# A four-batch mixture-of-experts kernel: the next batch's routing among a batch's last three tiles, its exponentials behind the first two evictions of x

## The reference, cut to what matters

```
# x (4, 1024, 1024) f32, side (4, 1024, 1), cond (4, 1024); E = 8 experts, F = 128, R = 16, top 2
def cond_ref(side, cond, x, k):                 # k = 10240, for each of 16 (here 4) matrices
    att = softmax(x, axis=-1) / sqrt(1024)
    adj = side * cond[:, None, :] * att
    adj[:, diag, diag] = -inf
    return 1.0 at the k largest entries of each matrix, 0.0 elsewhere
def ffn(m):                                     # m: the 0/1 mask of above, (4, 1024, 1024)
    scores = softmax(m @ G); w = top-2 of scores, at their experts
    gated = silu(m @ gate_w[e].T) * (m @ up_w[e].T)
    out  = sum over e of w[e] * gated @ down_w[e].T
    out += sum over e of w[e] * (m @ lora_A[e].T) @ lora_B[e].T
    return out
result = x + ffn(cond_ref(side, cond, x, 10240))
```

## Time and profile before

| | us |
|---|---|
| median of three runs | 833.69 |
| lowest and highest | 831.17, 837.47 |
| the profiled execution | 836.23 |
| its span, first to last instruction | 834.5 |
| mean granted TensorE clock, as a share of full | 0.838 |

### The profile page before, as it was taken

How to read it: one execution, slowest core, us unless ns; L and a number is a source line. 1 busy time by engine, 2 the same in 40 slices (tenths; PEclk the granted TensorE clock), 3 DMA queues, 4 the chain that set the end, 5 groups by cost and what they waited for, 6 DMA issues and landing times.

```text
span 834.5 us, 14610 instructions
## 1 busy us (share of the span) xinstructions
PE 529.9 (63%) x4178; PEld 358.9 (43%) x4178; DVE 519.5 (62%) x1242; ACT 455.4 (55%) x655; POOL 388.8 (47%) x337
## 2 busy tenths in 40 slices
PE   0211376289888754787887726987788368798810
PEld 0200365156555533454555414654455146465500
DVE  5768799576778465865885676757861623233335
ACT  6686387658744564485444553874445345355510
POOL 7123200234473114487786124877871157767510
PEclk9755599589999995898899967999999869899965
DMA  9980340114232904478377734685678247767569
GB/s 315 358 234 0 115 189 26 45 55 158 88 127 86 356 28 129 147 252 288 107 263 240 319 104 148 215 287 174 212 247 334 77 131 252 268 212 264 203 234 380
DMA packets 80443, 159.93 MB, mean 192 GB/s; under 512 B 22889, under 2 KB 32105, under 8 KB 79856
## 3 DMA queue, kind: packets, MB, share of 16 engines
q1 hardware_dynamic: 59760, 108.60, 37.8%
q0 software_dynamic: 20608, 50.37, 17.3%
HBM read 107.53 MB, written 73.40 MB: 217 GB/s over the span
## 4 chain that ended last, share of the span: by engine, by line
DMA 19%; PE 18%; DVE 17%; issue 15%; POOL 14%; ACT 8%; DVEq 4%; SPq 3%; POOLq 1%; ACTq 0%
DMA out_dram<-piece 7%; DMA piece<-put_rows 6%; PE pa L676 5%; ACT mask L791 3%; DMA xg<-mask_rows,where 3%; POOL piece L526 3%; POOL piece L529 3%; DVE mask L1060 3%; DVE w L1166 2%; PE pb L663 2%; POOL xg L509 2%; ACT t_row L828 2%; DMA w<-put_rows 2%; PE pd L625 2%; POOL put_rows L517 2%
## 5 line engine op out<-in xcount | busy, mean ns | idle before, releaser
L676 PE MATMUL pa<-w,xt 128*128 x1472 | 203.2, 294 | 1.1 <-issue 0.9
L848 ACT ACTIVATE y<-pc,where 128x512 f32<-128x512 f32 x184 | 125.3, 687 | 104.8 <-PE pc L702 97.4
L676 PEld LDWEIGHTS pa<-w,xt 128*128 128x128 f16 x1472 | 150.7, 103 | 62.1 <-issue 14.7
L517 POOL DMA_INDIRECT put_rows<-y,where x92 | 92.5, 1005 | 151.9 <-ACT y L848 133.3
L1336 DVE SCALAR_TENSOR_TENSOR g_full<-pa,where,s_act 128x144 f32<-128x144 f32 x92 | 33.5, 365 | 197.0 <-ACT s_act L840 196.9
L509 POOL DMA_INDIRECT xg<-mask_rows,where x92 | 97.4, 1058 | 122.8 <-DVEq L1328 92.9
L835 ACT ACTIVATE xt<-pb 128x1024 f16<-128x1024 f16 x92 | 94.3, 1025 | 101.7 <-PE pb L663 98.7
L663 PE MATMUL pb<-ident,xg 128*128 128x128 f16 x736 | 61.4, 231 | 68.5 <-DMA xg<-mask_rows,where 46.2
L663 PEld LDWEIGHTS pb<-ident,xg 128*128 128x128 f16 x736 | 48.7, 104 | 80.1 <-DMA xg<-mask_rows,where 53.5
L840 ACT ACTIVATE s_act<-pa,small 128x128 f32<-128x128 f32 x92 | 33.8, 368 | 86.8 <-PE pa L676 86.8
L702 PE MATMUL pc<-lb,gt 128*128 x184 | 77.4, 420 | 0.0
(11 more groups left out here) (208 smaller groups left out, 880.0 us busy)
## 6 DMA issues: line engine op xcount, KB each, us to landing
piece<-put_rows SPq DMA_DIRECT2D x96, 256.0 KB
v<-in_x_dram SPq DMA_DIRECT2D x40, 512.0 KB, 9.1
piece<-in_x_dram SPq DMA_DIRECT2D x48, 256.0 KB
out_dram<-piece SPq DMA_DIRECT2D x48, 256.0 KB, 3.8
mask_rows<-mask SPq DMA_DIRECT2D x4, 2048.0 KB, 16.6
w<-put_rows SPq DMA_DIRECT2D x16, 512.0 KB, 10.2
w<-in_L_ffn_gate_w_dram SPq DMA_DIRECT2D x8, 512.0 KB, 10.2
w<-in_L_ffn_up_w_dram SPq DMA_DIRECT2D x8, 512.0 KB, 8.3
```

The lines of the kernel that those rows point to most:

```text
L517: pool.indirect_dma_start(out=put_rows[n % 2], out_offset=bass.IndirectOffsetOnAxis(ap=put_row[n][:, i:i + 1], axis=0), in_=y[:, g % NY, : ...
L676: last = pe.matmul(l1[g % 2], xt[:, g % 2, t, :], w1[:, bass.ds(e, 1), t, k, :].rearrange("p o n -> p (o n)"), start=(t == 0 and k == 0), ...
L848: nc.scalar.activation(y[:, g % NY, half * HALF:(half + 1) * HALF], pc[:, half, :], ACT.Copy, scale=y_scale[n][:, i:i + 1]).then_inc(y_rea ...
```

## The change

The search's steps move up by a third to one and a half tiles each; the turning of the mask goes from tiles 19 to 22 into tiles 17 to 19; the five parts of route get places of their own among tiles 20 to 22, with rank and place_slots on TensorE and the last score in tile 20; the probabilities go to tile 20; the maxima move to tiles 20 to 22, six of them into tile 22; the exponentials of batch n + 1 are issued at the start of batch n, behind its first two evictions of x (for n = 1 and 2); GpSimd issues the next batch's first gathers behind the put of tile 20; the sums of pieces skip tile 16, and the mask's move stands behind the load of piece 13.

```diff
--- before.py
+++ after.py
@@ -76,29 +76,36 @@
     SCALE_AT = {(0, 0): 0, (0, 1): 1, (0, 2): 2, (1, 0): 3, (1, 1): 4, (1, 2): 5, (2, 0): 6, (2, 1): 7}
     SIDE_SUM_AT = (1, 3)
     DIAG_AT = 3
-    AIM_AT = {(2, 2): 1, (5, 1): 2, (8, 0): 3, (10, 1): 4}
+    AIM_AT = {(2, 2): 1, (5, 1): 2, (7, 2): 3, (9, 2): 4}
     DVE_COUNT_AT = {(3, 1): (1, 0), (3, 2): (1, 1), (4, 0): (1, 2), (5, 2): (2, 0), (6, 0): (2, 1),
-                    (6, 1): (2, 2), (8, 0): (3, 0), (8, 1): (3, 1), (8, 2): (3, 2)}
+                    (6, 1): (2, 2), (7, 2): (3, 0), (8, 0): (3, 1), (8, 1): (3, 2)}
     ACT_COUNT_AT = {(3, 0): (1, 0), (3, 1): (1, 1), (3, 2): (1, 2), (4, 0): (1, 3), (5, 2): (2, 0),
-                    (6, 0): (2, 1), (6, 1): (2, 2), (6, 2): (2, 3), (8, 1): (3, 0), (8, 2): (3, 1),
-                    (9, 0): (3, 2), (9, 1): (3, 3)}
-    SUM_AT = {(5, 0): 1, (7, 2): 2, (10, 0): 3}
-    BELOW_AT = {10: (0, 2), 11: (4,), 12: (6, 7)}
-    DVE_BELOW_AT = {(10, 1): 1, (11, 1): 3, (12, 1): 5}
-    BEST_AT = {(10, 2): 0, (11, 0): 1, (11, 2): 2, (12, 0): 3, (12, 2): 4, (13, 0): 5, (13, 1): 6, (13, 2): 7}
-    NEAREST_AT, NEAREST_SPREAD_AT = (14, 1), (14, 3)
-    RANK_AT = {(15, 0): (0, 1), (15, 1): (2, 3)}
-    PICK_AT, PICK_SUM_AT = (15, 2), (16, 0)
-    MASK_AT = {(16, 1): (0, 1), (16, 2): (2, 3), (17, 0): (4, 5), (17, 1): (6, 7)}
-    MASK_SUM_AT = (18, 1)
-    CHECK_AT = (18, 2)
-    TURN_AT = {(19, 0): 0, (19, 2): 1, (20, 0): 2, (20, 2): 3, (21, 0): 4, (21, 2): 5, (22, 0): 6, (22, 2): 7}
-    STORE_MT_AT = dict(TURN_AT)
-    MAX_AT = {(19, 2): 0, (20, 0): 1, (20, 1): 2, (20, 2): 3, (21, 0): 4, (21, 2): 5, (22, 0): 6, (22, 2): 7}
-
-
-    PIECE_AT = {**{j + 1: j for j in range(9)}, **{j + 4: j for j in range(9, PIECES)}}
-    PIECES_FIRST = 14
+                    (6, 0): (2, 1), (6, 1): (2, 2), (6, 2): (2, 3), (8, 0): (3, 0), (8, 1): (3, 1),
+                    (8, 2): (3, 2), (9, 0): (3, 3)}
+    SUM_AT = {(5, 0): 1, (7, 1): 2, (9, 2): 3}
+    BELOW_AT = {10: (0, 2), 11: (4, 6), 12: (7,)}
+    DVE_BELOW_AT = {(10, 0): 1, (11, 0): 3, (12, 0): 5}
+    BEST_AT = {(10, 1): 0, (10, 2): 1, (11, 0): 2, (11, 1): 3, (11, 2): 4, (12, 0): 5, (12, 1): 6, (12, 2): 7}
+    NEAREST_AT, NEAREST_SPREAD_AT = (13, 0), (13, 2)
+    RANK_AT = {(14, 0): (0, 1), (14, 1): (2, 3)}
+    PICK_AT, PICK_SUM_AT = (14, 2), (15, 0)
+    MASK_AT = {(15, 1): (0, 1), (15, 2): (2, 3), (16, 0): (4, 5), (16, 1): (6, 7)}
+    MASK_SUM_AT = (16, 3)
+    CHECK_AT = (17, 0)
+    TURN_AT = {(17, 1): 0, (17, 3): 1, (18, 0): 2, (18, 2): 3, (18, 3): 4, (19, 0): 5, (19, 2): 6, (19, 3): 7}
+    STORE_MT_AT = {(17, 1): 0, (17, 2): 1, (18, 0): 2, (18, 1): 3, (18, 2): 4, (19, 0): 5, (19, 1): 6, (19, 2): 7}
+    LAST_SCORE_AT = (20, 1)
+
+    CHOOSE_AT, WEIGH_AT, PLACE_AT, TABLE_AT, SLOTS_TAKEN_AT = (20, 1), (21, 0), (21, 0), (21, 1), (22, 0)
+    PAIR_RANK_AT, SLOTS_AT = (20, 3), (22, 0)
+    PROBS_AT = (20, 2)
+
+    MAX_AT = {(20, 2): (0,), (21, 2): (1,), (22, 1): (2, 3, 4), (22, 2): (5, 6, 7)}
+    EXPS_FIRST = 0
+
+
+    PIECE_AT = {**{j + 1: j for j in range(9)}, **{j + 4: j for j in range(9, 12)}, **{j + 5: j for j in range(12, PIECES)}}
+    PIECES_FIRST = 12
 
     with ExitStack() as ctx:
         def sb(name, shape, dt):
@@ -529,11 +536,15 @@
                 nc.gpsimd.tensor_tensor(piece[:, at, 0, :], piece[:, at, 0, :], piece[:, at, 2, :],
                                         ALU.add).then_inc(summed_piece, 1)
 
-            for n in range(B):
+            def first_gathers(n):
                 pool.wait_ge(routed, n + 1)
                 pool.wait_ge(mask_stored, 16 * (n + 1))
                 for i in range(NX):
                     gather(n, i)
+
+            for n in range(B):
+                if n == 0:
+                    first_gathers(0)
                 if n >= 2:
 
                     pool.wait_ge(summed_piece, PIECES * (n - 1))
@@ -549,8 +560,11 @@
                             below_third(n + 1, q)
                     if n > 0 and i in PIECE_AT:
                         sum_piece(n - 1, PIECE_AT[i])
-                for i in range(T - 3, T):
-                    put_out(n, i)
+                put_out(n, T - 3)
+                if n + 1 < B:
+                    first_gathers(n + 1)
+                put_out(n, T - 2)
+                put_out(n, T - 1)
 
         @block.tensor
         def _(pe):
@@ -751,6 +765,12 @@
                         turn_mask(n + 1, c)
                         if c > 0:
                             score(n + 1, c - 1)
+                    if (i, spot) == LAST_SCORE_AT:
+                        score(n + 1, C - 1)
+                    if (i, spot) == PAIR_RANK_AT:
+                        rank(n + 1)
+                    if (i, spot) == SLOTS_AT:
+                        place_slots(n + 1)
 
                 for i in range(T):
                     experts[i] = load_expert(n, i)
@@ -765,15 +785,9 @@
                     if i >= 2:
                         second_layer(n, i - 2, experts[i - 2])
                     between(i, 3)
-                if more:
-                    score(n + 1, C - 1)
                 turn_g(n, T - 1)
                 second_layer(n, T - 2, experts[T - 2])
-                if more:
-                    rank(n + 1)
                 second_layer(n, T - 1, experts[T - 1])
-                if more:
-                    place_slots(n + 1)
 
         @block.scalar
         def _(act):
@@ -898,9 +912,17 @@
                         count(n + 1, k, p)
                     if more and (i, spot) in STORE_MT_AT:
                         store_mt(n + 1, STORE_MT_AT[i, spot])
+                    if more and (i, spot) == PROBS_AT:
+                        probabilities(n + 1)
+                        if n + 2 < B:
+                            for c in range(EXPS_FIRST):
+                                exponential(n + 2, c)
 
                 store_xt(n, 0)
                 store_xt(n, 1)
+                if n > 0 and more:
+                    for c in range(EXPS_FIRST, C):
+                        exponential(n + 1, c)
                 for i in range(T):
                     silu(n, i)
                     if i + 2 < T:
@@ -914,13 +936,8 @@
                     between(i, 2)
                 store_y(n, T - 2, 0)
                 store_y(n, T - 2, 1)
-                if more:
-                    probabilities(n + 1)
                 store_y(n, T - 1, 0)
                 store_y(n, T - 1, 1)
-                if n + 2 < B:
-                    for c in range(C):
-                        exponential(n + 2, c)
 
         @block.vector
         def _(dve):
@@ -1420,8 +1437,19 @@
                         make_mask(n + 1, MASK_AT[here])
                     if here == CHECK_AT:
                         check_mask(n + 1)
+                    if here == CHOOSE_AT:
+                        choose(n + 1)
+                    if here == WEIGH_AT:
+                        weigh(n + 1)
+                    if here == PLACE_AT:
+                        place_pairs(n + 1)
+                    if here == TABLE_AT:
+                        fill_table(n + 1)
+                    if here == SLOTS_TAKEN_AT:
+                        take_slots(n + 1)
                     if n + 2 < B and here in MAX_AT:
-                        maximum(n + 2, MAX_AT[here])
+                        for c in MAX_AT[here]:
+                            maximum(n + 2, c)
 
                 for i in range(T):
                     between(i, 0)
@@ -1431,8 +1459,6 @@
                         store_gt(n, i - 1)
                     between(i, 2)
                 store_gt(n, T - 1)
-                if more:
-                    route(n + 1)
 
 
             for c in range(C):
```

## The result

The kernel with the change takes 877.3 us (median of four runs, 868.4 to 880.1), the kernel before in the same comparison 832.8: a ratio of 1.051, 95% interval 1.042 to 1.060. The forecast was 856.0 with a range of 832 to 872. So the sign was right and the size was not: by the ratio it is about 42 slower, where 22 were forecast. The profiled execution took 875.1, its span 873.3; that of before had 836.2 and 834.5.

A forecast was written before the change was run, and what follows sets the result against it. An order of waits, not a full engine, was taken to bound the kernel. Boundary, search and turning +3.8, exponentials +13, pieces +2, clock and port +3 make +21.8 on 836.2, less 2.5: about 856 us, range 832 to 872.

The forecast's parts named there:

- What bounds it: Whole kernel: no engine is full, an order of waits bounds a batch; TensorE's 20.7 us stretch at three boundaries is targeted.
- From choose to the next first layer: Batch boundary: 6.2 us longer after batch 2, 9.6 after batches 0 and 1, which have maxima; 25.4 over three boundaries.
- Rival 2: Faster: exponentials vanish behind VectorE's scalings, maxima behind put and gather, boundary first layers run warm; 828.5 us, chance 0.12.
- The exponentials: Start of batches 1 and 2: they delay the first silu, tile 3 comes 6.5 us later in each; +13.
- The search, packed: Search up to the mask's check: two tiles' own VectorE work falls out, mask ready 3.5 us earlier per batch.
- clock and port: TensorE's second layers at the lower clock, and piece sums beside routing stretching VectorE's work: +3 us, bounds -5 and +9.
- The turning of the mask: Check to choose: blocks packed two, three, three into tiles 17 to 19 take 30.5 us, 3.7 less per batch.
- Pieces: GpSimd's sums of pieces waiting for loads in the last batch, less one sum before its last gather: +2 us.
- rival 4: Much slower: GpSimd stands at late-loaded pieces 14 and 15, y's two buffers stop ScalarE; 868 us and more, chance 0.12.
- The forecast's sign: Whole kernel: the change makes it slower than before, beyond what a measurement tells from no change; chance 0.70.
- The sum: Whole kernel: all terms together add 21.8 us to the profiled 836.2, giving 858.0, less 2.5 for the median.

## Why the prediction was right or wrong

**What bounds it: right.** That an order of waits sets a batch, and that the time saved from TensorE's idle stretch at the boundary would come back elsewhere, is what the traces show.

**From choose to the next first layer: right.** 34.5, 34.5 and 30.3 for 35.4, 35.4 and 32.3, with each of the named waits in place: TensorE at the table (5.84 for "some 7"), the maxima in threes ahead of the stores of gt, the gathers behind tile 20's put. The experiment with the maxima moved gives their price in this stretch by itself, 3.4 and 3.9. Rival 2, in which they vanish behind put and gather, falls. The forecast has a slip here: 35.4 less 26.1 is 9.3 and not 9.6, so the three boundaries add up to 24.8 and not 25.4; the runs gave 22.3.

**The exponentials: right in mechanism, somewhat less in size.** +6.4 in batch 1 for 6.5, +4.1 in batch 2: 10.5 at tile 3 and not 13. The terms named for the first silu add up to 12.9 (1.2, 1.28, 9.15, 1.28), not to the 13.3 written; it came at 12.5. The scalings took the 3.67 that was taken. Of the 13.7 that the two starts won with the exponentials in tile 20, 7.5 reached the end; some of the rest was paid behind choose. Of a drain at a switch of tables nothing is seen, as in the earlier trace rows.

**The search, packed: wrong, the larger miss.** The step said that what falls out is two tiles' own VectorE work, 1.36 each, with 0.8 of waits, and that the start of the best-of-row steps doesn't move: 3.5 earlier per batch. The check came 2.7 later in batch 0, 0.8 earlier in batch 1, 4.4 later in batch 2 (the change at tile 3 taken off). By the same stages, both halves failed. The start moved: the first best-of-row step is 3.3, 1.3 and 4.2 later, behind a tile 9 that waits 4.26 for ScalarE (batch 0; 3.2 and 2.8 in the others). With the sums in tile 10 it came 5.2, 0.5 and 1.6 earlier after the batch's first layer. From there to the check I took 3.5 off, and it is 0.6 less, 2.2 less and 0.2 more. That VectorE is nearly full there was right (busy 38.3 of 44.2, 43.3 of 48.2 and 41.6 of 45.8 before), and two gates did fall out. But the last step of the gates left takes 2.1, 5.4 and 4.5 more in that stretch, with 4.59 in each batch for the one beside GpSimd's pair of products; the two gates had given 2.7. The step put nothing for it: "clock and port", +3 for the whole kernel, had the port only for pieces beside routing.

What was shown: packing the search alone costs 3.3%, with next to no gain in its length; the stretched step changes with the place of the pair of products. What was not: that any one of the three waits (tiles 9, 12, 16) is the cause. Taking one away gave nothing clear of noise twice and a loss once, and all three together a loss, which the move of product 6 brings. A reading that fits the packed search alone is that the search is a chain through four engines whose length hardly depends on how many tiles share it, so that a tile taken out is a tile at full price elsewhere. Product 6 moved shows that its length does depend on what stands beside what: the check came 9.0, 4.3 and 4.9 later than in the packed search. No run packs the search and keeps GpSimd's products clear of VectorE's two-input steps, so how much of the miss is the port and how much the chain stays open.

**The turning of the mask: wrong.** Check to choose stayed at 33.8, 34.5 and 34.3, not 30.5. Tiles 18 and 19 were sized well, 21.0, 20.9 and 20.7 together for 20.2. So the step that failed is the 27.3 for tiles 17 to 19, which took 29.8, 30.5 and 30.3, and most of that is tile 17: forecast at 7.1, it took 8.8, 9.6 and 9.6. It follows the wait of 5.65 and starts at the lower clock (first layer 3.81 for 2.02). The rest of the stretch is 4.0 where 3.2 stood (3.6 less 0.4). And the stretch that I compared with, 34.2, was batch 2's alone; the mean of the three is 33.7. Alone and behind the unpacked search, the packed turning did save 2.0 of the 3.7, and lost 4.9 behind choose. The sign of the remedy was wrong too: I had seen that a block waits 1.95 for the eviction of the one before it, and still counted packing three to a tile as a gain, where spacing them gave 5 us per batch.

**Pieces: small, and better than forecast.** The last batch is 0.8 shorter, where +2 stood. The wait of rival 4 is there. GpSimd's timeline late in batch 2:

```profile
672.30 1.02 POOL L524 DMA_INDIRECT put_rows<-y,where  x1 [5.64 <-ACT y L862]
679.68 1.26 POOL L533 TENSOR_TENSOR piece<-piece 128x512 f32<-128x512 f32 x1 [6.36 <-DMA piece<-put_rows]
...
682.59 1.00 POOL L524 DMA_INDIRECT put_rows<-y,where  x1 [0.31 <-issue]
686.42 1.26 POOL L533 TENSOR_TENSOR piece<-piece 128x512 f32<-128x512 f32 x1 [2.83 <-DMA piece<-put_rows]
```

Piece 14's sum waits 6.36 for its load (5.93 in batch 1) and piece 15's 2.83, with a put behind each. But ScalarE, which was to stop for its two buffers of y, waits only for TensorE ahead of evictions of y in that stretch, never for a put:

```profile
679.39 0.69 ACT L862 ACTIVATE y<-pc,where 128x512 f32<-128x512 f32 x1 [2.25 <-PE pc L716]
686.17 0.69 ACT L862 ACTIVATE y<-pc,where 128x512 f32<-128x512 f32 x1 [0.21 <-PE pc L716]
```

So rival 4's time came about (868 and more), by another way than its own: a hit of its number would have been luck. The forecast's sign was not luck: the boundary and the exponentials, forecast at +38.4, gave +32.6.

**The sum.** Of the 17 by which the span's change of 38.8 lies above 21.8, the search gives +16.7 and the turning +12.5; the boundary (-3.1), the exponentials (-2.7), the pieces (-2.8), the clock's separate term (-3, which lies inside the others) and the prologue (-0.5) give back 12.1, which leaves 17 within the rounding.

## What to carry to other kernels

A stretch that is a chain of waits need not get shorter when tiles between its steps are taken out. Here it did not, and the tiles came back at full price behind it. Before packing steps, look at which of them will then run beside each other. When a step waits in a hand-written queue, ask what stands behind it: here one block turned behind each second layer gave 1.3%, where packing cost time, because TensorE then has work during the wait. A small matmul moved the same way gave too little to tell by itself. Price each part of a change alone if you can; here the packed search (3.3%) and the packed turning (1.0%), each sensible, cost time by themselves.

## What the runs showed of the hardware that was not expected

A VectorE operation with two inputs in SBUF can last until the end of two whole products of GpSimd that follow each other: 0.31 becomes 4.59 and 1.27 becomes 5.25. Beside one product the gate's last step took 0.47 to 2.98 in the traces before and after. MAX8, which reads one tensor, stays at 1.21 to 1.23 throughout. And the waits of 4.26 and 5.65 us on TensorE were dearer than their length: what stood behind them ran at the lower clock, a second-layer matmul 0.63 for 0.38 and the first layer 3.05 and 3.81 for 2.02.
